# Dividing the row-flag checks of a mixed megakernel's first chunk into scan, adds and comparison

## The reference, cut to what matters

```python
def step(carry, x):
    h, stopped = carry
    stop = jnp.logical_or(stopped, jnp.mean(x) == 0)
    logits = jnp.concatenate([x, h]) @ W_attn.T + b_attn
    aw = jax.nn.softmax(logits)
    applied = aw @ enc
    comb = jax.nn.relu(jnp.concatenate([x, applied]) @ W_comb.T + b_comb)
    h_new = jnp.tanh(comb @ W_ih.T + b_ih + h @ W_hh.T + b_hh)
    out = h_new @ W_out.T + b_out
    out = jnp.where(stop, jnp.zeros_like(out), out)
    h = jnp.where(stop, h, h_new)
    return ((h, stop), out)
```

## Time and profile before

| what | us |
|---|---|
| median of three runs | 1029.65 |
| lowest and highest of them | 1026.86 and 1033.49 |
| the profiled execution | 1031.62 |
| its span | 1029.7 |
| TensorE busy, of the span | 933.1 |
| VectorE busy | 723.2 |
| GpSimd busy | 564.1 |
| ScalarE busy | 478.0 |

### The profile page before, as it was taken

One profiled execution on the slowest core, in us unless ns is written; L12 is line 12 of the kernel. 1 busy time (PEld: TensorE's weight loads), 2 busy tenths in 40 slices (PEclk: granted clock), 3 DMA queues, 4 the chain that ended last, 5 costly groups with the idle time before them and its releaser, 6 DMA issues. The chain is left out here.

```text
span 1029.7 us, 31937 instructions
## 1 busy us (share of the span) xinstructions
PE 933.1 (91%) x13408; PEld 739.6 (72%) x13408; DVE 723.2 (70%) x1818; ACT 478.0 (46%) x895; POOL 564.1 (55%) x516
## 2 busy tenths in 40 slices
PE   3498998999999999999998988999999999998786
PEld 3376876777877887778776866777777777777454
DVE  5635566876867677676779655878878778778564
ACT  2233322423232323223332226778787778777652
POOL 4688821334343434334354555766776867767673
PEclk9655555999999999999999998999999999999997
DMA  9220007342322222122233420000000000000001
GB/s 253 45 78 22 2 1 153 97 114 69 83 62 66 82 67 84 45 83 67 83 85 103 117 71 1 3 3 3 4 3 3 3 3 3 3 3 3 3 1 42
DMA packets 46532, 51.81 MB, mean 50 GB/s; under 512 B 22165, under 2 KB 37302, under 8 KB 46390
## 3 DMA queue, kind: packets, MB, share of 16 engines
q1 hardware_dynamic: 43472, 48.78, 18.1%
q10 hardware_dynamic: 2918, 1.01, 0.5%
HBM read 48.20 MB, written 1.57 MB: 48 GB/s over the span
## 5 line engine op out<-in xcount | busy, mean ns | idle before, releaser
L746 POOL TENSOR_TENSOR ex<-ex,xn 128x512 f32<-128x512 f32 x128 | 164.0, 1282 | 247.4 <-ACT thcb L999 160.2
L999 ACT ACTIVATE thcb<-ps 128x512 f32<-128x512 f32 x132 | 78.9, 598 | 204.5 <-PE ps L1834 198.6
L832 POOL TENSOR_TENSOR wu<-encC,wu 128x1024 f16<-128x1024 f32 x64 | 135.6, 2134 | 27.2 <-ACT encC L1071 27.0
L1849 PE MATMUL ps<-ex,wd 128*128 128x256 f32 x512 | 140.3, 396 | 1.3 <-POOL ex L746 0.9
L1417 DVE SCALAR_TENSOR_TENSOR ex<-thcb,ps 128x512 f32<-128x512 f32 x132 | 90.6, 686 | 49.1 <-ACT thcb L999 44.5
L1834 PE MATMUL ps<-xnT,wg 128*128 128x256 f16 x768 | 106.5, 275 | 1.5 <-DVE ex L1423 1.4
L826 POOL TENSOR_TENSOR wd<-wd,a_sum 128x512 f32<-128x512 f32 x64 | 66.7, 1044 | 72.8 <-DVE a_sum L1544 72.6
L1834 PE MATMUL ps<-xnT,wu 128*128 128x256 f16 x768 | 106.1, 275 | 0.0
L1903 PE MATMUL ps<-wg,M 128*128 128x128 f16 x1536 | 98.5, 222 | 2.0 <-DVE wg L1513 2.0
L1903 PEld LDWEIGHTS ps<-wg,M 128*128 128x128 f16 x1536 | 93.2, 99 | 6.8 <-DVE wg L1513 2.4
L1774 PEld LDWEIGHTS ps<-eb,encC 128*128 128x128 f16 x3072 | 86.7, 98 | 14.1 <-DVE eb L1285 7.3
(11 more groups left out here) (321 smaller groups left out, 1783.0 us busy)
## 6 DMA issues: line engine op xcount, KB each, us to landing
xn<-coef_rows SPq DMA_DIRECT2D x128, 256.0 KB, 3.9
thcb<-in_L_ffn_Wg SPq DMA_DIRECT2D x8, 256.0 KB, 4.1
thcb<-in_L_ffn_Wu SPq DMA_DIRECT2D x8, 256.0 KB, 3.1
wd<-in_L_ffn_Wd SPq DMA_DIRECT2D x2, 1024.0 KB, 9.8
xtok<-in_x SPq DMA_DIRECT2D x4, 256.0 KB, 5.7
thcb<-in_ctx SPq DMA_DIRECT2D x2, 512.0 KB, 11.1
wu<-in_L_xcond_attn_wq SPq DMA_DIRECT2D x2, 512.0 KB, 11.1
wu<-in_L_xcond_attn_wk SPq DMA_DIRECT2D x2, 512.0 KB, 10.8
```

Source lines behind the costliest of these rows:

```text
L746: nc.gpsimd.tensor_tensor(hid[:, side(m, n), :], gu[:, side(m, n), :], other, ALU.mult)\
L832: nc.gpsimd.tensor_tensor(z[:, 1, 8 * u:8 * u + 8, :], a_Zc[:, u], z[:, 0, 8 * u:8 * u + 8, :], ALU.subtract)\
L999: nc.scalar.activation(th[:, side(m, n), :], bank(side(m, n)), ACT.Tanh, scale=0.5 / WSCALE)\
L1849: last = mm(bank(5)[:, half * HT:(half + 1) * HT], wd[:, 2 * q + p, :], hid[:, side(m, n), p * HT:(p + 1) * HT], start=(n == 0 and p == 0) ...
```

## The change

`STOPS` gets new keys, and `stops` is divided: scan, adds and comparison of a chunk are three entries with a gap each. The instructions stay the same. Chunk 0's scan moves to gap 9 (step 2, place 1), its adds to 13, its comparison to 15, sum0 to 17, count0 to 18 and keep0 to 21. Chunk 1's three parts stand at 37, 41 and 43, chunk 2's at 45, 47 and 49, chunk 3's at 53, 55 and 57. The final sum, count and keep stay where they are.

```diff
-        STOPS = {26: 0, 27: "sum0", 28: "count0", 30: "keep0", 39: 1, 51: 2, 58: 3, 59: "sum", 61: "count", 62: "keep", GAPS + 9: "scales"}
+        STOPS = {9: ("scan", 0), 13: ("adds", 0), 15: ("flags", 0), 17: "sum0", 18: "count0", 21: "keep0",
+                 37: ("scan", 1), 41: ("adds", 1), 43: ("flags", 1), 45: ("scan", 2), 47: ("adds", 2), 49: ("flags", 2),
+                 53: ("scan", 3), 55: ("adds", 3), 57: ("flags", 3), 59: "sum", 61: "count", 62: "keep", GAPS + 9: "scales"}
...
-                if isinstance(p, int):
-                    dve.wait_ge(s["exact_ready"], (p + 1) * 17)
+                b4 = scan.rearrange("p (n k x) -> p n k x", k=4, x=32)[:, :, :, 31]
+                if isinstance(p, tuple) and p[0] == "scan":
+                    dve.wait_ge(s["exact_ready"], (p[1] + 1) * 17)
                     settle(V.tensor_tensor_scan(scan, blockmask[:, :],
-                                                cen[:, :, :].rearrange("p n d -> p (n d)")[:, p * CT:(p + 1) * CT],
+                                                cen[:, :, :].rearrange("p n d -> p (n d)")[:, p[1] * CT:(p[1] + 1) * CT],
                                                 0.0, mul, add))
-                    b4 = scan.rearrange("p (n k x) -> p n k x", k=4, x=32)[:, :, :, 31]
+                elif isinstance(p, tuple) and p[0] == "adds":
                     settle(V.tensor_tensor(bsum[:, 0, :], b4[:, :, 0], b4[:, :, 1], add))
                     settle(V.tensor_tensor(bsum[:, 1, :], bsum[:, 0, :], b4[:, :, 2], add))
                     settle(V.tensor_tensor(bsum[:, 0, :], bsum[:, 1, :], b4[:, :, 3], add))
-                    settle(V.tensor_scalar(flags[:, p * TPC:(p + 1) * TPC], bsum[:, 0, :], 0.0, None, ALU.is_equal))
+                elif isinstance(p, tuple):
+                    settle(V.tensor_scalar(flags[:, p[1] * TPC:(p[1] + 1) * TPC], bsum[:, 0, :], 0.0, None, ALU.is_equal))
```

## The result

The changed kernel takes 1034.34 us, median of 19 runs (1030.94 to 1037.77); the kernel before, 19 runs beside it, 1031.99 (1026.86 to 1033.9). The ratio is 1.0034 with a 95% interval of 1.0019 to 1.0048: slower by 2.0 to 5.0 us. A second set of the two kernels gave 1.0039 (1.0014 to 1.0065). So the change costs about a third of a per cent.

A forecast was written before the change was run, and what follows sets the result against it. Chunk 0's serial step loop was taken as the bound, with TensorE hardly idle after it. Additions of 10.1 us less 4.6 saved gave +5.5 on the 1029.65 us median, 1035.2 us; the 8-in-10 range was 1029.2 to 1040.8.

The forecast's parts named there:

- scan in step 2: At gap 9 the scan waits for GpSimd's chunk 0, then its next instruction: `comb` 2.6 us late, between 1.75 and 2.85.
- adds 0: Three VectorE adds at gap 13 in step 3, partly beside GpSimd: 0.4 us uncovered, between 0 and 1.15.
- sum0, count0, keep0: Gaps 17, 18 and 21: sum0 0.1 us, count0's four uncovered TensorE matmuls in step 4 0.9, keep0 0 or 0.2.
- step 6 relieved: Check 0 with sum0 no longer stands ahead of step 7's `nmax`; step 6 becomes like step 5, 3.25 us saved.
- scan 1 and adds 1, less check 1's saving: Steps 9 and 10, VectorE's cover used up: scan at gap 37 1.35 us, adds at gap 41 1.5, less 0.36 saved.
- cover of place 1: VectorE's idle time before `comb` during the 48 matmuls, 1.11 or 1.12 us in steps 2 to 4; work fitting there is free.
- higher sum: Rival: every scan and add in chunk 0's steps is held off by GpSimd; +11.0 us, 1040.7 us, chance 0.10.
- lower sum without the port: Rival: GpSimd does not slow VectorE's scans and adds, which take their shortest times; +2.2 us, 1031.9 us, chance 0.11.
- Check 1's saving of 0.36: Step 10's `nmax` at 118.75 could have started at 118.39 without check 1 ahead of it: 0.36 us saved.
- it arrives at the end whole: After chunk 0 TensorE hardly idles, so a microsecond won or lost in chunk 0 should reach the kernel's end whole.
- the steps are paced by setup matmuls alone: Rival: TensorE's setup matmuls behind `comb` pace the steps, hiding everything there but count0; -3.7 us, 1026.0 us, chance 0.05.
- the delay is absorbed: Rival: chunk 0's delay vanishes later in the kernel; 1029.7 us, chance 0.06.

## Why the prediction was right

It said 1035.2 us, +5.5 us, +0.5%, and no change by the measure of 1%. The steps gave +5.26 us and the runs a ratio of 1.0034 and 1.0039, 3.5 and 4.0 us. Term by term:

| term | predicted, us | measured, us |
|---|---|---|
| scan in step 2 | +2.6 | +2.37 |
| adds 0 | +0.4 | +0.14 |
| sum0, count0, keep0 | +1.0 | +0.78 |
| step 6 relieved | -3.25 | -3.23 |
| scan 1 and adds 1, less check 1's saving | +2.49 | +2.81 |
| scan 2 | +1.6 | +1.76 |
| comparison 2 | +0.2 | +0.20 |
| scan 3 | +1.25 | +1.26 |
| comparison 3, less check 3's saving | -0.78 | -0.84 |

**The scan in step 2** went as worked out: `comb` stood behind a wait of 1.42 us and behind the GpSimd instruction that had been issued just before. The delay is about 1.42 + 2.04 us less the 1.11 of cover. The Trainium skill (SBUF — State Buffer, "Who interferes with whom") says that the order of issue decides who blocks whom. The two orders are both here: 2.04 for the scan behind GpSimd, and 1.22 with GpSimd's 2.22 where the scan came first.

**The cover of place 1** was the right reading. Where it had idle time (steps 3 and 4), adds and sum0 fitted; from step 9 on they did not, and nearly all of their length went into the step. The higher sum, with a collision at every add, +11, missed: adds 0 met GpSimd once, adds 1 once. The lower sum without the port, +2.2, falls by the scans of 2.04, 1.54 and 1.79 us and by the steps; the interval of the runs alone, 2.0 to 5.0 us, holds it.

**Check 1's saving of 0.36 was wrong.** I had read that `nmax` at 118.75 was late by 0.36 and counted that as won. But TensorE, too, has a queue in place 0 of that step. In the kernel before:

```profile
117.65 0.63 PE L1763 MATMUL ps<-w_attnT,Hc 128*32 128x128 f32 x2
118.21 2.07 PE L1730 MATMUL ps<-wu 64*128 64x128 f32 x8
120.22 0.31 PE L1767 MATMUL ps<-ident,en 32*128 32x32 f32 x1
```

The transpose comes 2.57 us after the logits matmul, right behind eight setup matmuls (late setup work that hangs at that place). In the changed kernel, where `nmax` is in time, it is 2.57 too:

```profile
119.64 0.63 PE L1767 MATMUL ps<-w_attnT,Hc 128*32 128x128 f32 x2
...
122.21 0.31 PE L1771 MATMUL ps<-ident,en 32*128 32x32 f32 x1
```

An `nmax` that is 0.36 late was hidden there; what was in the way was the setup group. The version with every piece in place 2 or 3 shows it as well: its step 9 is 0.36 shorter and its step 10 0.42 longer than before. Against that version scan 1 and adds 1 cost 1.38 us (9.21 less 7.83) and 1.37 (9.12 less 7.75), close to the 1.35 and 1.5 taken; the +2.81 in the table is larger than +2.49 because the saving is missing. In step 14 the same reading was right, for place 0 of step 15 holds no setup group.

**That it arrives at the end whole** is shown for part of the way. Within the two first profiles the distance of equal instructions stays at 5.86 to 5.88 us from step 24 (at 225 us) to step 51 (at 424 us); no stretch in between absorbs it. Of this distance 0.46 us lay between the two executions before the first `nmax`, 5.26 is chunk 0, and 0.20 comes in step 23 (8.03 in place of 7.83), for which no run gives a cause. Then the profiled execution of the kernel before is slower: its step 51 takes 10.27 us at a granted clock of 0.83, that of the changed kernel 8.73 at 1.00. By the end it has lost some 6 us against the other in all, which is why its span is no shorter. Whether such dips average out over many runs is not shown. The measured 2.0 to 5.0 us ends just below 5.27, the second set's 1.4 to 6.7 holds it, and the middles, 3.5 and 4.0, both lie below. Whether the changed kernel gains something like a microsecond back on average is open; ten profiles don't tell.

**Where luck helped.** The 1035.2 us stand on the median of three runs, 1029.65. The 19 runs of the same kernel beside the changed one have 1031.99, and from there +5.5 would be 1037.5; so that 1034.34 lies this near owes 2.3 us to a low base. How often a piece would meet GpSimd was estimated between bounds, not derived: step 3 with the same adds at the same gap grew by 0.14, but by 0.53 and 0.98 in the two experiments that moved scan 0 or took its wait away, and step 2 grew by 2.37, but by 3.03 in two versions with the same scan at the same gap. That the sum came within 0.3 us of the steps is in part chance.

The rivals: nothing here supports that the steps are paced by setup matmuls alone (steps 9 to 13 all grew; one place, place 0 of step 10, was paced by them, and it cost the saving of 0.36), nor that the delay is absorbed.

## What to carry to other kernels

Divide a block of side work only into places where its engine waits, and count at each place what is already there: the same piece was free in front of `nmax` and cost nearly its whole length in front of `comb` (scan 3: nothing against 1.26 us). A piece that must wait for another engine's chain goes well behind the chain's end, not at it. And where a saving is read from one late instruction, look whether the next engine in the loop would have been ready to use it.

## What the runs showed of the hardware that was not expected

A VectorE instruction that waits for a GpSimd instruction's end by semaphore lost the port to GpSimd's next instruction, issued without a wait, each time: 2.04 us for the scan in all four profiles that have it at gap 9 behind this wait, never 1.22. Four-column instructions suffer as much as wide ones: an add of 0.17 us alone took up to 1.23.

GpSimd's chunk and the recurrence keep no fixed distance. In the two profiles of the kernel before, the chunk ends 1.60 and 1.37 us after `eb`. VectorE stood 1.39 and 1.42 us for it in the two profiles of the changed kernel and 2.07 in those of two versions that are the same up to there, which moved step 2 by 0.66 us. Whether those 0.66 come from the version or from the execution, single profiles do not tell.

The granted clock rises at the start of the expert units at different moments of the same work, from within step 17 to within step 18. The Trainium skill (TensorE: Matmul & The Clock Gate, "Part 1: The HAM clock gate (the "warmup" mystery)") says that the same kernel shows different counts of slow matmuls at its start from run to run. Here it is the start of the expert units in the midst of a kernel, and the 0.79 and 0.50 of step 17 in two executions of one kernel are of that kind. The spread of runs, 7 us in the first set and 8 to 9 in the second, is not much larger than the 5.3 us that steps 17, 18 and 21 can make.
